# Head attention: the scores of two key tiles as four 32-row matmuls side by side, then twelve value products

## The chip, the cores and the metric

The kernel runs on one core of one Trainium2 chip. The metric is the device time of one execution in microseconds, the median over the runs shown. Lower is better.

## The reference

The program is a small network on x of 4 x 1024 tokens with 128 features: a mixture-of-experts layer, **head attention**, a second mixture-of-experts layer, a recurrent layer, a decayed attention with an MLP, and a recurrent layer again. The change lies in head attention alone, which the reference states so (`x` is already the layer norm of the residual stream, and the result is added to it):

```python
def _L0_attn_ref(x, weight):            # x: 4, 1024, 128
    nh = 16
    hs = c // nh                        # 8
    y = x.reshape(b, t, nh, hs).transpose(0, 2, 1, 3)
    scores = jnp.einsum('bhtk,bhsk->bhts', y, y) / math.sqrt(hs)
    attn = jax.nn.softmax(scores, axis=-1)
    o = jnp.einsum('bhts,bsc->bhtc', attn, x)
    return o.transpose(0, 2, 1, 3).reshape(b, t, nh * c) @ weight
```

So there are 4 x 16 = 64 heads of 8 dimensions. Each makes a 1024 x 1024 matrix of weights, which multiplies all 128 features of x, and each head's result of 128 x 1024 goes through its own 128 x 128 block of `weight` into the sum.

## The kernel before

Features lie on the 128 partitions, tokens along the free dimension. Single precision is rebuilt from two parts: every operand is split into a high part (rounded to the matmul's input type) and a low part (the rest), and `product` (L89 to L94) does three matmuls: low x high, high x low, high x high. Its lines L92, L93 and L94 are those that the profile names for value and output products.

`head_attention` first runs a layer norm (lines below L300, labelled `heads_norm`), which also writes the high and low parts to DRAM (`heads_parts`). Then comes one block in which the engines run their own programs, written out by hand and joined by semaphores. The work is 64 heads (`COUNT`), numbered h, of 8 key tiles of 128 keys (`TILES`), numbered s; n = 8h + s counts the tiles. The 1024 queries are two halves of 512, one PSUM bank each.

- **SP** (the queue that issues DMAs). `load_head(h)` (L722 to L728) fetches the operands of the scores of head h: 8 dimensions have 8 high and 8 low rows, 16 rows of 1024 numbers, and two such sets lie in `left` (high, low; high, low) and two in `right` (high, low; low, high), so that 32 rows carry all four products of parts. That is four DMAs of 64 KB (L727). The other 96 partitions of both tiles hold zeros, set once by GpSimd (L888, L889), for which SP waits before the first load. In the loop over heads SP waits for the reciprocals of head h (`inverse_ready`), stores them to DRAM in four DMAs (L737), waits until the scores of head h are done, loads head h+2, waits until the stores have landed, and loads the reciprocals back, broadcast to all partitions, as `scale` (L744).
- **TensorE**, step n: `scores(h, s)` (two matmuls, one for each half, L766) into one of two pairs of PSUM banks; where s is 7 and h at least 2, `add_head(h-2)`, the output product of a finished head (six matmuls); and then `weighted_rows` for the tile seven steps back (`TRAIL = 7`), six matmuls of the value product into the two OUT banks. Tile 0 of a head waits until the row products of the head before have read these banks (`scaled_ready`).
- **ScalarE**: the exponential of a tile (L817, 1024 columns at once, with the sum over queries in `accum_out`), where s is 0, 2, 4 or 6 (`ACT_HIGH`) also its high part (L822), and at the end of a head the high parts of u for the head before (L807). There are four buffers of exponentials; tile n waits for the low part of tile n - 4.
- **VectorE**: the high part of the other tiles (L871), the low part of all (L873). Behind tile 5 (`TRAIL - 2`) of head h it waits for the scale and for the last value product of head h-1 and multiplies the two (`scale_sums`, the row products u, L841); behind tile 7 the low parts of u (L847); and before tile 0 of the next head the reciprocals of the sums (L831) and their transpose (L834), which signals `inverse_ready`.

The attention is symmetric in its scores, so that the sum over queries of a key's row equals the sum that the softmax needs for that key as a query; this is why the scale comes after the value product.

Of the kernel before, what the change touches and what calls it, by code (L numbers as in the profile page):

```python
# [16 lines left out]
P = 128  # L17
BATCH, T = 4, 1024
TOKENS = BATCH * T
BANK = 512  # L20
CHUNKS = TOKENS // BANK
HALVES = T // BANK
# [10 lines left out]
HEADS, HEAD = 16, 8  # L33
TILES = T // P
# [24 lines left out]
def after(eng, sem, count):  # L59

    if isinstance(count, int) and count <= 0:
        return
    eng.wait_ge(sem, count)
# [9 lines left out]
def f(ap):  # L73

    return ap.bitcast(F32)
# [590 lines left out]
def head_attention(nc, tag, psum, consts, dram, x):  # L666


    with ExitStack() as ctx:
        sb, sem = sb_in(ctx, nc), sems_in(ctx, nc, tag)  # L670
# [6 lines left out]
        parts_dram = nc.dram_tensor(f"{tag}_parts", (P, 3, TOKENS), F32, kind="Internal").ap()  # L677
# [15 lines left out]

        zeroed, heads_loaded = sem("zeroed"), [sem("heads_even"), sem("heads_odd")]
        turned, v_by_act, v_by_dve = sem("turned"), sem("v_by_act"), sem("v_by_dve")
# [6 lines left out]
        sum_done, added = sem("sum_done"), sem("added")  # L702
        HEAD_LOADS = 4
        ACT_HIGH = (0, 2, 4, 6)
        TRAIL = 7
        COUNT = BATCH * HEADS
# [12 lines left out]
        with nc.Block() as block:  # L719
            @block.sync  # L720
            def _(sp):
                def load_head(h):  # L722
                    at = slice(h // HEADS * T, (h // HEADS + 1) * T)
                    dims = slice(h % HEADS * HEAD, (h % HEADS + 1) * HEAD)
                    for tile, orders in ((left, (0, 0)), (right, (0, 1))):
                        for i, order in enumerate(orders):
                            sp.dma_start(f(tile[i * 2 * HEAD:(i + 1) * 2 * HEAD, h % 2, :]),  # L727
                                         parts_dram[dims, order:order + 2, at]).then_inc(heads_loaded[h % 2], 16)  # L728

                sp.wait_ge(zeroed, 2)  # L730
                load_head(0)
# [16 lines left out]
            def _(pe):  # L748
# [11 lines left out]

                def scores(h, s):
                    if s == 0:
                        pe.wait_ge(heads_loaded[h % 2], 16 * HEAD_LOADS * (h // 2 + 1))
                    after(pe, exp_done, h * TILES + s - 1)
                    for half in range(HALVES):
                        last = pe.matmul(psum[:, SCORES + 2 * (s % 2) + half, :], left[:, h % 2, s * P:(s + 1) * P],  # L766
                                         right[:, h % 2, half * BANK:(half + 1) * BANK], start=True, stop=True)
                    last.then_inc(scores_done, 1)

# [20 lines left out]
                pe.wait_ge(v_by_dve, VALUE_BANKS)  # L790
                for n in range(COUNT * TILES + TRAIL):
                    if n < COUNT * TILES:
                        scores(n // TILES, n % TILES)
                    if n % TILES == TRAIL and n // TILES >= 2:
                        add_head(n // TILES - 2)
                    if n >= TRAIL:
                        weighted_rows((n - TRAIL) // TILES, (n - TRAIL) % TILES)
                for g in (COUNT - 2, COUNT - 1):
# [29 lines left out]
            def _(dve):  # L828
# [32 lines left out]
                for n in range(COUNT * TILES):  # L861
# [11 lines left out]
                    dve.tensor_tensor(e_lo[:, s, :], e[:, s % 4, :], f(e_hi[:, s, :]), ALU.subtract).then_inc(low, 1)  # L873
                    if s == TRAIL - 2 and h >= 1:
                        scale_sums(h - 1)
# [8 lines left out]
                dve.wait_ge(added, BATCH * HALVES)  # L884

            @block.gpsimd
            def _(pool):
                pool.memset(f(right[:, :, :]), 0.0).then_inc(zeroed, 1)  # L888
                pool.memset(f(left[:, :, :]), 0.0).then_inc(zeroed, 1)  # L889

# [685 lines left out]
```

## Time and profile before

| | |
|---|---|
| median of 3 runs | 3015.69 us (3014.63 to 3017.92) |
| the profiled execution | 3016.72 us, span 3014.9 us |
| busy over the span: TensorE, VectorE, ScalarE, GpSimd | 89%, 77%, 60%, 32% |
| head attention, first scores to last row products | 697 to 1727 us |
| mean granted TensorE clock, whole span | 0.929 |

The span is the time from the first to the last instruction on the core. A granted clock of 1 is 2.4 GHz, 0.5 is 1.2 GHz, and a number between is a mean over time. Matmuls are pipelined: a row with x2 merges two that overlap, and the time of one says less than the distance between starts. "PEld" is the weight load of TensorE, which runs beside its matmuls. "SPq" rows are DMA issues: the time that the queue's sequencer takes to issue one, not the transfer. In a view of waits, the name behind the arrow is what ended the wait.

### The profile page before, as it was taken

How to read it: one execution, taken by the hardware profiler on the slowest of the kernel's cores; microseconds unless marked ns; L12 is line 12 of the kernel's file. 1: busy time of each engine (PE TensorE's matmuls, PEld its weight loads, DVE VectorE, ACT ScalarE, POOL GpSimd, SP SyncE). 2: the span in 40 equal slices, each digit the busy share in tenths (PEclk: the TensorE clock that was granted, in tenths of full speed). 3: DMA queues.
4: the chain of work that ended last, by engine and by line, in shares of the span. 5: the costliest groups of instructions: out<-in, count | busy, mean ns of one | idle time of the engine just before them, and what ended most of it. 6: DMA issues, size and time to landing. Idle time of an engine off the chain costs nothing. (4 is left out here: it accounts for less than half of the span.)

```text
span 3014.9 us, 37679 instructions
## 1 busy us (share of the span) xinstructions
PE 2673.9 (89%) x11635; PEld 2163.0 (72%) x11635; DVE 2308.4 (77%) x3342; ACT 1804.5 (60%) x2927; POOL 965.2 (32%) x761
## 2 busy tenths in 40 slices
PE   7799999988999999999999978999999884555678
PEld 5688777866888888888888756887878663344456
DVE  6677777867999999999999776777877547776555
ACT  3355554547888888888888634555545443443365
POOL 2466666650000000000000034666666403444310
PEclk8899999998999999999999988999999886777788
DMA  1566655632111111111111106665656000000000
GB/s 55 128 142 132 152 123 122 146 99 76 44 52 53 50 46 53 53 45 51 53 53 43 46 25 144 132 151 126 147 128 140 21 22 28 14 14 0 8 7 28
DMA packets 76820, 222.76 MB, mean 74 GB/s; under 512 B 12145, under 2 KB 16881, under 8 KB 76529
## 3 DMA queue, kind: packets, MB, share of 16 engines
q1 hardware_dynamic: 76432, 220.77, 29.7%
q8 instruction: 70, 1.15, 0.2%
q14 instruction: 94, 0.76, 0.1%
q10 hardware_dynamic: 224, 0.07, 0.0%
HBM read 205.87 MB, written 10.75 MB: 72 GB/s over the span
## 5 line engine op out<-in xcount | busy, mean ns | idle before, releaser
L629 POOL TENSOR_TENSOR moe_experts_lo<-moe_experts_hidden,moe_experts_hi 128x512 fp32r<-128x512 f32 x512 | 662.3, 1294 | 388.3 <-ACT moe_experts_hi L567 388.3
L873 DVE TENSOR_TENSOR heads_e_lo<-heads_e,heads_e_hi 128x1024 fp32r<-128x1024 f32 x512 | 624.4, 1220 | 75.3 <-ACT heads_e_hi L822 66.4
L817 ACT ACTIVATE heads_e<-psum 128x1024 f32<-128x1024 f32 x512 | 525.0, 1025 | 131.2 <-PE psum L766 131.1
L574 ACT ACTIVATE psum<-psum 128x512 f32<-128x512 f32 x512 | 298.0, 582 | 493.6 <-PE psum L94 493.6
L601 DVE TENSOR_TENSOR moe_experts_weighted<-moe_experts_spread,psum 128x512 f32<-128x512 f32 x512 | 351.3, 686 | 238.2 <-PE psum L94 181.2
L92 PE MATMUL psum<-moe_n_hi,moe_w_lo 128*128 128x512 f32 x1024 | 406.2, 397 | 38.0 <-DVE moe_experts_hidden L606 34.2
L93 PE MATMUL psum<-moe_n_lo,moe_w_hi 128*128 128x512 f32 x1024 | 404.5, 395 | 0.0
L94 PE MATMUL psum<-moe_n_hi,moe_w_hi 128*128 128x512 f32 x1024 | 403.9, 394 | 0.0
L92 PE MATMUL psum<-heads_e_hi,heads_v_lo 128*128 128x512 f32 x1024 | 400.5, 391 | 0.7 <-DVE heads_u L841 0.7
L94 PE MATMUL psum<-heads_e_hi,heads_v_hi 128*128 128x512 f32 x1024 | 399.5, 390 | 0.0
L93 PE MATMUL psum<-heads_e_lo,heads_v_hi 128*128 128x512 f32 x1024 | 399.1, 390 | 0.0
L606 DVE TENSOR_TENSOR moe_experts_hidden<-moe_experts_weighted,psum 128x512 f32<-128x512 f32 x512 | 352.0, 687 | 34.3 <-POOL moe_experts_lo L629 16.9
L282 POOL CAST moe_router_hi<-moe_norm_raw 128x128 fp32r<-128x128 f32 x2 | 0.6, 291 | 1058.3 <-DMA moe_norm_raw<-in_router 1058.3
L567 ACT CAST moe_experts_hi<-moe_experts_hidden 128x512 fp32r<-128x512 f32 x512 | 314.0, 613 | 34.9 <-DVE moe_experts_hidden L606 34.9
L766 PE MATMUL psum<-heads_right,heads_left 128*128 128x512 f32 x1024 | 318.7, 393 | 4.8 <-ACT heads_e L817 3.9
L822 ACT CAST heads_e_hi<-heads_e 128x1024 fp32r<-128x1024 f32 x256 | 269.6, 1053 | 8.1
L92 PEld LDWEIGHTS psum<-moe_n_hi,moe_w_lo 128*128 128x128 f32 x1024 | 195.8, 191 | 84.0 <-DVE moe_experts_hidden L606 38.1
L766 PEld LDWEIGHTS psum<-heads_right,heads_left 128*128 128x128 f32 x1024 | 192.8, 189 | 48.0 <-ACT heads_e L817 7.4
L94 PEld LDWEIGHTS psum<-moe_n_hi,moe_w_hi 128*128 128x128 f32 x1024 | 195.9, 191 | 41.4
L93 PEld LDWEIGHTS psum<-moe_n_lo,moe_w_hi 128*128 128x128 f32 x1024 | 196.1, 192 | 40.8
L92 PEld LDWEIGHTS psum<-heads_e_hi,heads_v_lo 128*128 128x128 f32 x1024 | 192.6, 188 | 42.6 <-DVE heads_e_lo L873 1.1
L94 PEld LDWEIGHTS psum<-heads_e_hi,heads_v_hi 128*128 128x128 f32 x1024 | 192.5, 188 | 41.2
(426 smaller groups left out, 4527.2 us busy)
## 6 DMA issues: line engine op xcount, KB each, us to landing
moe_experts_spread<-moe_mask SPq DMA_DIRECT2D x128, 1024.0 KB, 11.5
heads_scale<-heads_inverse_copy SPq DMA_DIRECT2D x64, 512.0 KB, 3.7
heads_left<-heads_parts SPq DMA_DIRECT2D x128, 64.0 KB
heads_right<-heads_parts SPq DMA_DIRECT2D x128, 64.0 KB
moe_experts_raw<-in_gate SPq DMA_DIRECT2D x16, 256.0 KB, 12.0
moe_experts_raw<-in_up SPq DMA_DIRECT2D x16, 256.0 KB
moe_experts_raw<-in_down SPq DMA_DIRECT2D x16, 256.0 KB
heads_parts<-heads_e_hi SPq DMA_DIRECT2D x16, 256.0 KB, 3.2
```

What stands on the lines that cost most here:

```text
L92: pe.matmul(out, w_lo, x_hi, start=first, stop=False, skip_group_check=True)
L93: pe.matmul(out, w_hi, x_lo, start=False, stop=False, skip_group_check=True)
L94: return pe.matmul(out, w_hi, x_hi, start=False, stop=last, skip_group_check=True)
L567: act.copy(hi[:, p, :], hidden[:, p % 2, :]).then_inc(high_ready, 1)
L574: act.activation(psum[:, GATE + p % 2, :], psum[:, GATE + p % 2, :], ACT.Silu).then_inc(silu_ready, 1)
L601: dve.tensor_tensor(weighted[:, p % 2, :], spread[:, pair % 2, p, j * BANK:(j + 1) * BANK], psum[:, UP + p % 2, :], ALU.mult).then_inc(wei ...
L606: dve.tensor_tensor(hidden[:, p % 2, :], weighted[:, p % 2, :], psum[:, GATE + p % 2, :], ALU.mult).then_inc(hidden_ready, 1)
L629: pool.tensor_tensor(lo[:, p, :], hidden[:, p % 2, :], f(hi[:, p, :]), ALU.subtract).then_inc(low_ready, 1)
L766: last = pe.matmul(psum[:, SCORES + 2 * (s % 2) + half, :], left[:, h % 2, s * P:(s + 1) * P], right[:, h % 2, half * BANK:(half + 1) * BA ...
L817: act.activation(e[:, s % 4, :], wide, ACT.Exp, scale=HEAD ** -0.5, accum_out=sums[:, h % 2, s:s + 1]).then_inc(exp_done, 1)
L822: act.copy(e_hi[:, s, :], e[:, s % 4, :]).then_inc(act_high, 1)
L873: dve.tensor_tensor(e_lo[:, s, :], e[:, s % 4, :], f(e_hi[:, s, :]), ALU.subtract).then_inc(low, 1)
```

## The change

Four things change, all inside the block of `head_attention`.

1. `left` and `right` get four copies of the 32 operand rows, on partitions 0, 32, 64 and 96, in place of one copy and zeros. `load_head` issues 16 DMAs in place of 4, all of the old shape (`HEAD_LOADS = 16`). The memsets and the wait for them go.
2. TensorE goes by pairs of tiles. `scores` makes four matmuls, two tiles by two halves, each with 32 rows of the array of its own (`rows`) and a PSUM bank of its own, and now waits until both tiles of the pair before have been read by the exponential. Behind them stand the value products of two tiles, twelve matmuls, six and five tiles back (`TRAIL = 6`); `add_head` stands behind the scores of tiles 6 and 7.
3. ScalarE makes the high parts of the odd tiles, VectorE those of the even ones.
4. VectorE's row products stand behind tile 5 as before (`TRAIL - 1`).

```diff
--- before.py
+++ after.py
@@ -691,7 +691,7 @@
         u_hi, u_lo = sb(f"{tag}_u_hi", [P, 2, HALVES, BANK], F32R), sb(f"{tag}_u_lo", [P, 2, HALVES, BANK], F32R)
         SCORES, OUT, SUM = 0, 4, 6
 
-        zeroed, heads_loaded = sem("zeroed"), [sem("heads_even"), sem("heads_odd")]
+        heads_loaded = [sem("heads_even"), sem("heads_odd")]
         turned, v_by_act, v_by_dve = sem("turned"), sem("v_by_act"), sem("v_by_dve")
         scores_done, exp_done, dve_high, act_high, low = (
             sem("scores"), sem("exp"), sem("dve_high"), sem("act_high"), sem("low"))
@@ -700,9 +700,9 @@
         scale_loaded = [sem("scale_even"), sem("scale_odd")]
         out_done, scaled_ready, u_high, u_low = sem("out"), sem("scaled"), sem("u_high"), sem("u_low")
         sum_done, added = sem("sum_done"), sem("added")
-        HEAD_LOADS = 4
-        ACT_HIGH = (0, 2, 4, 6)
-        TRAIL = 7
+        HEAD_LOADS = 16
+        ACT_HIGH = (1, 3, 5, 7)
+        TRAIL = 6
         COUNT = BATCH * HEADS
         VALUE_BANKS = TOKENS // BANK
 
@@ -724,10 +724,11 @@
                     dims = slice(h % HEADS * HEAD, (h % HEADS + 1) * HEAD)
                     for tile, orders in ((left, (0, 0)), (right, (0, 1))):
                         for i, order in enumerate(orders):
-                            sp.dma_start(f(tile[i * 2 * HEAD:(i + 1) * 2 * HEAD, h % 2, :]),
-                                         parts_dram[dims, order:order + 2, at]).then_inc(heads_loaded[h % 2], 16)
-
-                sp.wait_ge(zeroed, 2)
+                            for g in range(4):
+                                row = 32 * g + i * 2 * HEAD
+                                sp.dma_start(f(tile[row:row + 2 * HEAD, h % 2, :]),
+                                             parts_dram[dims, order:order + 2, at]).then_inc(heads_loaded[h % 2], 16)
+
                 load_head(0)
                 load_head(1)
                 for h in range(COUNT):
@@ -759,13 +760,17 @@
                     last.then_inc(sum_done, 1)
 
                 def scores(h, s):
+
                     if s == 0:
                         pe.wait_ge(heads_loaded[h % 2], 16 * HEAD_LOADS * (h // 2 + 1))
-                    after(pe, exp_done, h * TILES + s - 1)
-                    for half in range(HALVES):
-                        last = pe.matmul(psum[:, SCORES + 2 * (s % 2) + half, :], left[:, h % 2, s * P:(s + 1) * P],
-                                         right[:, h % 2, half * BANK:(half + 1) * BANK], start=True, stop=True)
-                    last.then_inc(scores_done, 1)
+                    after(pe, exp_done, h * TILES + s)
+                    for tile in (s, s + 1):
+                        for half in range(HALVES):
+                            g = 2 * (tile % 2) + half
+                            rows = slice(32 * g, 32 * (g + 1))
+                            last = pe.matmul(psum[:, SCORES + g, :], left[rows, h % 2, tile * P:(tile + 1) * P],
+                                             right[rows, h % 2, half * BANK:(half + 1) * BANK], start=True, stop=True)
+                        last.then_inc(scores_done, 1)
 
                 def weighted_rows(h, s):
                     pe.wait_ge(low, h * TILES + s + 1)
@@ -788,13 +793,14 @@
                     last.then_inc(turned, 1)
                 pe.wait_ge(v_by_act, VALUE_BANKS)
                 pe.wait_ge(v_by_dve, VALUE_BANKS)
-                for n in range(COUNT * TILES + TRAIL):
+                for n in range(0, COUNT * TILES + TRAIL, 2):
                     if n < COUNT * TILES:
                         scores(n // TILES, n % TILES)
-                    if n % TILES == TRAIL and n // TILES >= 2:
-                        add_head(n // TILES - 2)
                     if n >= TRAIL:
-                        weighted_rows((n - TRAIL) // TILES, (n - TRAIL) % TILES)
+                        if n % TILES == TRAIL and n // TILES >= 2:
+                            add_head(n // TILES - 2)
+                        for m in (n - TRAIL, n - TRAIL + 1):
+                            weighted_rows(m // TILES, m % TILES)
                 for g in (COUNT - 2, COUNT - 1):
                     add_head(g)
 
@@ -871,7 +877,7 @@
                         dve.tensor_copy(e_hi[:, s, :], e[:, s % 4, :]).then_inc(dve_high, 1)
                         dve.wait_ge(dve_high, high_dve)
                     dve.tensor_tensor(e_lo[:, s, :], e[:, s % 4, :], f(e_hi[:, s, :]), ALU.subtract).then_inc(low, 1)
-                    if s == TRAIL - 2 and h >= 1:
+                    if s == TRAIL - 1 and h >= 1:
                         scale_sums(h - 1)
                     if s == TILES - 1 and h >= 1:
                         u_lows(h - 1)
@@ -882,11 +888,6 @@
                 u_lows(COUNT - 1)
                 add_batch(BATCH - 1)
                 dve.wait_ge(added, BATCH * HALVES)
-
-            @block.gpsimd
-            def _(pool):
-                pool.memset(f(right[:, :, :]), 0.0).then_inc(zeroed, 1)
-                pool.memset(f(left[:, :, :]), 0.0).then_inc(zeroed, 1)
 
 
 def recurrent_layer(nc, tag, psum, consts, dram, x, out=None):
```

On TensorE, this stood where a head's last scores are followed by the output product of an older head (`heads_u`, `heads_w`) and the first value product of its own (`heads_e`, `heads_v`), before:

```order
L766 MATMUL psum<-heads_right,heads_left 128x512 x2
L92 MATMUL psum<-heads_e_hi,heads_v_lo 128x512
L93 MATMUL psum<-heads_e_lo,heads_v_hi 128x512
L94 MATMUL psum<-heads_e_hi,heads_v_hi 128x512
L92 MATMUL psum<-heads_e_hi,heads_v_lo 128x512
L93 MATMUL psum<-heads_e_lo,heads_v_hi 128x512
L94 MATMUL psum<-heads_e_hi,heads_v_hi 128x512
L766 MATMUL psum<-heads_right,heads_left 128x512 x2
L92 MATMUL psum<-heads_u_hi,heads_w_lo 128x512
```

and now, the four scores of tiles 6 and 7 and the six matmuls of the output product behind them:

```order
L771 MATMUL psum<-heads_right,heads_left 128x512 x4
L92 MATMUL psum<-heads_u_hi,heads_w_lo 128x512
L93 MATMUL psum<-heads_u_lo,heads_w_hi 128x512
L94 MATMUL psum<-heads_u_hi,heads_w_hi 128x512
L92 MATMUL psum<-heads_u_hi,heads_w_lo 128x512
L93 MATMUL psum<-heads_u_lo,heads_w_hi 128x512
L94 MATMUL psum<-heads_u_hi,heads_w_hi 128x512
L92 MATMUL psum<-heads_e_hi,heads_v_lo 128x512
```

Scores came two at a time between six products; they now come four at a time between twelve, or eighteen where the output product stands.

On the SP queue, the loads of heads 0 and 1 and then the loop's first head, before:

```order
L727 DMA heads_left<-heads_parts 16x1x1024 x2
L727 DMA heads_right<-heads_parts 16x1x1024 x2
L727 DMA heads_left<-heads_parts 16x1x1024 x2
L727 DMA heads_right<-heads_parts 16x1x1024 x2
L737 DMA heads_inverse_copy<-heads_inverse_rows 8x32 x4
L727 DMA heads_left<-heads_parts 16x1x1024 x2
L727 DMA heads_right<-heads_parts 16x1x1024 x2
L744 DMA heads_scale<-heads_inverse_copy 128x1024
```

and now:

```order
L729 DMA heads_left<-heads_parts 16x1x1024 x8
L729 DMA heads_right<-heads_parts 16x1x1024 x8
L729 DMA heads_left<-heads_parts 16x1x1024 x8
L729 DMA heads_right<-heads_parts 16x1x1024 x8
L738 DMA heads_inverse_copy<-heads_inverse_rows 8x32 x4
L729 DMA heads_left<-heads_parts 16x1x1024 x8
L729 DMA heads_right<-heads_parts 16x1x1024 x8
L745 DMA heads_scale<-heads_inverse_copy 128x1024
```

Between the stores of a head's reciprocals and the load of its scales stand 16 loads in place of 4. The order of the three kinds is the same.

On VectorE, from a head's row products (`heads_u`) to the transpose that ends the next, now:

```order
L847 TENSOR_TENSOR heads_u<-heads_scale,psum 128x512 x2
L877 CAST heads_e_hi<-heads_e 128x1024
L879 TENSOR_TENSOR heads_e_lo<-heads_e,heads_e_hi 128x1024 x2
L853 TENSOR_TENSOR heads_u_lo<-heads_u,heads_u_hi 128x512 x2
L837 RECIPROCAL heads_inverse<-heads_sums 128x8
L840 STREAM_TRANSPOSE heads_inverse_rows<-heads_inverse 128x32
```

Before, the same instructions stood there, with the cast between the two low parts.

## Rows read from the trace of the kernel before

**Rows 1.** Busy time by engine inside head attention: stretch, us, then PE, PEld, DVE, ACT, POOL.

```profile
720.00:1700.00 980.00, 979.34 (x4299) 806.41 (x4298) 909.07 (x1112) 845.40 (x1354) 0.00 (x0) 1.00 0.15 50
```

**Rows 2.** Waits by engine and line, 720 to 1700 us: total us, times, longest.

```profile
ACT heads_e L817 <- PE psum L766: 126.9, 246, 0.9
DVE heads_e_lo L873 <- ACT heads_e_hi L822: 60.3, 116, 0.5
```

**Rows 3.** Timeline of TensorE at 1214 us: start, us, instruction, count.

```profile
1214.02 0.39 PE L93 MATMUL psum<-heads_e_lo,heads_v_hi 128*128 128x512 f32 x1
1214.25 0.39 PE L94 MATMUL psum<-heads_e_hi,heads_v_hi 128*128 128x512 f32 x1
1214.47 0.62 PE L766 MATMUL psum<-heads_right,heads_left 128*128 128x512 f32 x2
1214.93 0.39 PE L92 MATMUL psum<-heads_e_hi,heads_v_lo 128*128 128x512 f32 x1
```

**Rows 4.** Timeline of VectorE: row products, end of a head, next row products.

```profile
1202.60 1.28 DVE L841 TENSOR_TENSOR heads_u<-heads_scale,psum 128x512 f32<-128x512 f32 x2
...
1208.23 0.21 DVE L834 STREAM_TRANSPOSE heads_inverse_rows<-heads_inverse 128x32 f32<-128x32 f32 x1
...
1218.56 1.28 DVE L841 TENSOR_TENSOR heads_u<-heads_scale,psum 128x512 f32<-128x512 f32 x2
```

**Rows 5.** Timeline of the SP queue, the same head.

```profile
1208.47 1.28 SPq L737 DMA_DIRECT2D heads_inverse_copy<-heads_inverse_rows  x4
1209.80 1.39 SPq L727 DMA_DIRECT2D heads_left<-heads_parts  x2
1211.23 1.35 SPq L727 DMA_DIRECT2D heads_right<-heads_parts  x2
1212.68 0.38 SPq L744 DMA_DIRECT2D heads_scale<-heads_inverse_copy  x1
```

**Rows 6.** Timeline of the weight loads at 1214 us.

```profile
1214.70 0.19 PEld L92 LDWEIGHTS psum<-heads_e_hi,heads_v_lo 128*128 128x128 f32 x1
```

**Rows 7.** Timeline of TensorE: one-column matmuls in a row, in the layer norm.

```profile
659.69 2.73 PE L208 MATMUL psum<-inv,heads_norm_squares 128*128 128x1 f32 x24
```

**Rows 8.** The tile of left operands: its load issues, ns min/median/max.

```profile
L727 SPq DMA_DIRECT2D heads_left<-heads_parts x128: 654/670/1155, 690.7 to 1689.4; - x128
```

**Rows 9.** The DRAM copy of the reciprocals: issues, ns min/median/max, and landing, us.

```profile
L737 SPq DMA_DIRECT2D heads_inverse_copy<-heads_inverse_rows x256: 263/288/917, 713.0 to 1719.8; - x128
L744 SPq DMA_DIRECT2D heads_scale<-heads_inverse_copy x64: 342/382/444, 717.2 to 1721.0; - x64
...
DMA to landing us min/median/max: 3.3/3.7/5.5
```

**Rows 10.** Line L834: the transpose that ends a head, ns, first and last start us.

```profile
L834 DVE STREAM_TRANSPOSE heads_inverse_rows<-heads_inverse x64: 211/211/213, 712.8 to 1718.6; 128x32 f32<-128x32 f32 x64
```

**Rows 11.** Timeline of the SP queue: the first eight loads, two pairs of four shown.

```profile
690.73 1.53 SPq L727 DMA_DIRECT2D heads_left<-heads_parts  x2
...
695.10 1.35 SPq L727 DMA_DIRECT2D heads_right<-heads_parts  x2
```

**Rows 12.** Waits of the SP queue, whole span: the one before the first load.

```profile
SPq L727 <- POOL heads_left L889: 3.6, 1, 3.6
```

**Rows 13.** DMA issues: a 64 KB load of another layer, KB, median us to landing.

```profile
cell_norm_raw<-in_wi SPq DMA_DIRECT2D x2, 64.0 KB, 2.0
```

**Rows 14.** Timeline of TensorE: the first scores, and what it waited for.

```profile
697.30 1.17 PE L766 MATMUL psum<-heads_right,heads_left 128*128 128x512 f32 x4 [0.83 <-ACT heads_v_lo L811]
```

**Rows 15.** Timeline of TensorE: after a long wait in the first layer.

```profile
105.97 0.80 PE L92 MATMUL psum<-moe_n_hi,moe_w_lo 128*128 128x512 f32 x1 [8.29 <-DVE moe_experts_hidden L606]
```

**Rows 16.** Stretches behind that wait: the column after POOL is the granted clock.

```profile
106.00:113.00 7.00, 7.00 (x20) 5.57 (x21) 3.95 (x6) 2.78 (x5) 2.92 (x3) 0.63 1.02 210
113.00:120.00 7.00, 7.00 (x33) 5.79 (x32) 4.51 (x7) 3.71 (x7) 4.75 (x4) 1.00 0.14 35
```

## The prediction

> **What bounds the kernel now.** I read the busy time by stretch first. Between 720 and 1700 us, inside head attention, TensorE is busy 979.34 of 980 us at a granted clock of 1.00, while VectorE has 909.07 and ScalarE 845.40 [rows 1]. So TensorE sets the pace of this stage. The waits say the same: ScalarE waits 126.9 us for scores and VectorE 60.3 us for ScalarE's high parts [rows 2], and TensorE has no wait worth a row. The transpose that ends a head starts first at 712.8 and, for the 64th head, at 1718.6 [rows 10]: (1718.6 - 712.8) / 63 = 15.97 us is the period of a head.
>
> The view that decides the forecast is the SP queue, since the change puts four times as many loads there. In one head [rows 5]: the transpose of VectorE starts at 1208.23 and takes 0.21 [rows 4], so the reciprocals are ready at 1208.44. SP issues four stores from 1208.47, then the four loads of head h+2 from 1209.80, and only then, at 1212.68, the broadcast load of the scales of head h. It lands 3.7 us after its issue (3.3 to 5.5) [rows 9], so at 1216.38. VectorE needs it for its row products at 1218.56 [rows 4]. **The slack is 2.2 us a head.** The reader should see that this queue is idle most of the time (from 1213.1 until the next head's stores, one period after 1208.47), and that nevertheless its latency lies 2.2 us under the critical path.
>
> **TensorE's part.** In a row, matmuls of 512 columns start 0.227 us apart, products and scores alike: 1214.02, 1214.25, 1214.47 for the first of two scores, 1214.93 for what follows both [rows 3]. A head has 48 value products, 6 output products and 16 score matmuls: 70 x 0.227 = 15.9 us, the measured period. The change makes the 16 into four groups of four on separate rows. No row shows such a group, so I bound its time S from both sides. Below: all four side by side cost one distance, 0.227. Above: nothing overlaps. The rest of the last product runs out (0.39 - 0.227 = 0.16), a weight load takes 0.19 [rows 6], the four start 0.227 apart (0.68), the last takes 0.39 and the next product's weight load 0.19: 1.61. Weight loads and one-column matmuls in a row go at 2.73 / 24 = 0.114 us each [rows 7], so between the ends I take four starts 0.114 apart with the weight loads hidden, about 0.45. TensorE's work per head is then 54 x 0.227 + 4S = 12.3 + 1.8 = 14.1 us, with ends of 13.2 and 18.7, against 15.9 now.
>
> The Trainium skill (TensorEngine Tiling (Array Packing), Key Properties) says that a change of tiling mode drains TensorE, and this change switches eight times a head. Worked out with drains on both sides and overlapping matmuls, S is 0.16 + 0.19 + 3 x 0.114 + 0.39 + 0.19 = 1.27 and a head 17.3 us, slower than now instead of faster. No run here shows such a switch between row groups. Whether 14.1 or 17.3, the sum below stays as it is, since something else takes 22.2 us; the rule decides only if that falls away, and there it is a rival.
>
> **VectorE and ScalarE.** Their instructions per head are the same (four high parts each; the even ones move to VectorE, the odd to ScalarE). Priced at nothing, covered by the stall found below: its cover is several us a head. VectorE's own floor is 15.97 less its waits, 60.3 us over 980 / 15.97 = 61.4 heads, 0.98: 14.99 us.
>
> **The SP queue.** A load issue takes 0.670 us (654 to 1155 ns) [rows 8], and eight in a row went from 690.73 to 696.45, 0.715 each with a long first one [rows 11]; in the steady head two take 1.43 and 1.35. I take 0.70. Each of the 16 new loads has the shape of the old ones, 16 rows of 4 KB, so twelve more issues are 12 x 0.70 = **8.4 us** ahead of the scale load. The waits for stored reciprocals and for free buffers that stand between them are over long before, and cost nothing. From reciprocals ready to scales landed:
> 0.03 + 1.33 (stores) + 2.88 (four loads) + 8.4 + 3.7 = 16.3 us, where it was 7.9.
>
> Now who waits. VectorE does its row products of head h behind its sixth tile of head h+1, as before. They are due 10.1 us after the reciprocals (1208.44 to 1218.56); the scales come at 16.3. In order behind them stand the tiles 6 and 7 of head h+1, the low parts of u and the reciprocals of head h+1, and only these release the next stores on SP. That is a closed loop. Its VectorE part is read off directly: row products at 1202.60, reciprocals ready at 1208.44, with no gap between, 5.84 us for the same instructions as after the change (one cast, two low parts, two of u, the reciprocal). With 0.05 for the wake-up the period is 16.3 + 0.05 + 5.84 = **22.2 us** a head instead of 15.97.
>
> Does anything else in this loop take longer? TensorE waits for the scaled rows before the first value product of head h+1, and must have done the last one before the next row products. That chain is 0.7 (first row product) + 48 x 0.227 + 3S = 0.7 + 10.9 + 1.4 = 13 us, 16.4 with S at 1.61. But TensorE will now idle 6 to 8 us each head. After a wait of 8.29 us [rows 15] the next 7 us had a mean granted clock of 0.63 [rows 16], which is 1.2 GHz for 74% of it, 5.2 us, and 2.4 GHz after that; 5.2 us of work at half the rate lose 2.6. So 16 us, at most 19, against 22.2: it is covered by 3 us or more. VectorE's tiles 4 and 5 hang on three groups of products: 0.7 + 3 x (2.72 + 0.45) + 2.6 + 1 for cold scores, then 2.3 for two exponentials, 1.1 for a cast and 1.2 for a low part, 18.4 us: covered too.
>
> **Start and end.** The memsets on GpSimd go, with the SP wait of 3.6 us for them [rows 12], so the first load is issued at 690.73 - 3.6 = 687.1. But head 0 now needs 16: the last is issued at 687.1 + 15 x 0.70 = 697.6 and lands 2.0 later (as a 64 KB load elsewhere [rows 13]), at 699.6, where scores begin at 697.30 now [rows 14]. With the scores exposed in pairs in that first head I take +3 us. The last two heads have no loads in front of their scales; between -1 and +4, I take +1.
>
> **Sum.** 62 heads have loads in front of their scales. 62 x (22.2 - 15.97) = 386; with 3 and 1, +390. The profiled execution took 3016.72 us (span 3014.9), so 3407, and the median of the runs is 1.0 lower: **3406 us**, 13% slower. A measurement of this kernel can tell 0.2%, 6 us, from no change.
>
> **Rivals.**
> 1. *The scales come later still*, or a chain through TensorE closes the loop. For it: the loads move 1 MB in 11 us right in front of the scale load, whose landing already varies to 5.5, and TensorE's margin is the smallest cover. Against: the scale load follows loads back to back today and lands in 3.7. At 5.5 each time the period is 24.0: 3016 + 62 x 8.0 + 4 = 3516. A TensorE held at half rate would need 48 x 0.454 + 3 x 1.7 + 0.7 = 27.6 us (3740), but then it wouldn't idle. Chance 0.12.
> 2. *Issues are cheaper in a long burst.* The nearest cheap rows are the scale issue at 0.382 and the stores at 0.288 [rows 9]. At 0.32, twelve are 3.8 us and the period 17.7: about 3125. Against: eight loads in a row went no faster than two. Chance 0.05, and 0.01 more that it just comes out even.
> 3. *The other side: the queue stays under the path* and TensorE's saving shows. That needs twelve issues within the slack, under 2.2 / 12 = 0.18 us each, where the shortest load is 0.654. Then VectorE bounds at 14.99: 3016 - 64 x 0.98 = 2953. The Trainium skill (TensorE: Matmul & The Clock Gate, Measured speedup vs the span model) gives 3.07 times for four row tiles of 512 columns, which would let that saving through; it says nothing of the queue. Chance 0.02.
> 4. *The drains bind*, by the rule above, with the queue out of the way: 3016 + 64 x (17.3 - 15.97) = 3101. Chance 0.01.
> 5. *The four matmuls don't run side by side.* Then S is 0.9 and nothing of the forecast changes; it is inside it.
>
> **How the numbers follow.** Forecast 0.79, rival 1 0.12, rival 2 0.05 and 0.01, rivals 3 and 4 0.02 and 0.01. The forecast's own ends: 0.66 an issue and 3.3 to land give 21.35 us a head and 3353; 0.715 with 4.5 to land gives 23.2 and 3468. Reaching into rival 1, the range is 3358 to 3505. Faster 0.02, within 0.2% 0.01, slower 0.97.
>
> **What would show it.** In the changed profile: the end-of-head transposes 22 us apart; SP with 16 loads in about 11.2 us between stores and scale issue; VectorE idle some 6 us before each row product, released by the scale load; TensorE at 60 to 70% busy in this stage with its idle time before a head's first value product, and a mean clock below 1. Wrong would be: issues under 0.6 us, row products released by TensorE, or a period under 20.

## The result, and the profile after

| | before | after |
|---|---|---|
| median of 4 runs | 3015.16 us (3014.28 to 3017.92) | 3413.43 us (3408.85 to 3421.34) |
| profiled execution, span | 3016.72, 3014.9 us | 3408.85, 3407.1 us |
| ratio, 95% interval | | 1.1322 (1.1299 to 1.1344) |
| period of a head, mean of the first 62 | 15.97 us | 22.33 us |

The change makes the kernel 13% slower. The forecast was 3406 us, range 3358 to 3505. The medians are of executions in the chip's usual state; one of the four of the version with one row group further down ran in a slower one, 3328.12 us at a mean granted clock of 0.807, and is left out of its median.

The page of the changed kernel, parts 1 and 2, shows no engine that got much more to do; TensorE is less busy and its clock lower in the stage:

```profile
PE 2745.8 (81%) x11635; PEld 2079.8 (61%) x11635; DVE 2338.4 (69%) x3342; ACT 1811.0 (53%) x2927; POOL 961.8 (28%) x759
...
PEclk8899999878888888888888889899999988677788
```

The same view as [rows 1], over the stretch 760 to 2050 us (stretch, its length, then busy PE, PEld, DVE, ACT, POOL, and the granted clock):

```profile
760.00:2050.00 1290.00, 997.79 (x4049) 688.31 (x4050) 881.03 (x1043) 802.51 (x1275) 0.00 (x0) 0.88 0.23 72
```

TensorE is busy 77% of the stage where it was 99.9%. The waits by engine and line, the view of [rows 2], name the chain:

```profile
PE psum L92 <- DVE heads_u L847: 292.2, 58, 6.4
ACT heads_e L823 <- PE psum L771: 289.8, 232, 5.1
DVE heads_u L847 <- DMA heads_scale<-heads_inverse_copy: 271.3, 58, 6.1
```

VectorE waits for the scale load before its row products, TensorE waits for the row products before a head's first value product, and ScalarE waits for the scores that stand behind that in TensorE's program. Of the three, the profile before had the wait of ScalarE, with 126.9 us over 980 [rows 2], that of TensorE once, with 0.7 us, and that of VectorE not at all. The tile of scales says how often, and how long its DMA takes:

```profile
  DMA heads_scale<-heads_inverse_copy: 291.0, 62
...
DMA to landing us min/median/max: 3.3/3.7/4.4
```

VectorE waited 62 times, once for each head that has loads in front of its scales, and the landing is as before, 3.7 us [rows 9]. One head on the SP queue, against [rows 5]:

```profile
1229.82 1.29 SPq L738 DMA_DIRECT2D heads_inverse_copy<-heads_inverse_rows  x4
1231.15 5.58 SPq L729 DMA_DIRECT2D heads_left<-heads_parts  x8
1236.77 5.54 SPq L729 DMA_DIRECT2D heads_right<-heads_parts  x8
1242.40 0.38 SPq L745 DMA_DIRECT2D heads_scale<-heads_inverse_copy  x1
1251.98 1.29 SPq L738 DMA_DIRECT2D heads_inverse_copy<-heads_inverse_rows  x4
```

and VectorE in the same head, against [rows 4]:

```profile
1246.11 1.28 DVE L847 TENSOR_TENSOR heads_u<-heads_scale,psum 128x512 f32<-128x512 f32 x2 [4.05 <-DMA heads_scale<-heads_inverse_copy]
...
1251.75 0.21 DVE L840 STREAM_TRANSPOSE heads_inverse_rows<-heads_inverse 128x32 f32<-128x32 f32 x1
```

The loop can be read off and closes: stores at 1229.82, loads at 1231.15 (1.33), scales at 1242.40 (11.25), row products at 1246.11 (3.71), reciprocals ready at 1251.96 (5.85), the next stores at 1251.98. That is 22.16 us. Over the whole stage the transpose that ends a head [rows 10] has

```profile
L840 DVE STREAM_TRANSPOSE heads_inverse_rows<-heads_inverse x64: 211/211/214, 714.7 to 2116.0; 128x32 f32<-128x32 f32 x64
```

and the 63rd of them starts at 2099.05, so 62 periods are 1384.3 us, 394.4 more than before. With the later first transpose (1.9 us) and 4.2 us less from the 63rd transpose to the end, that is the whole difference of the spans: 3014.9 + 1.9 + 394.4 - 4.2 = 3407.0.

What TensorE gained is there too, against [rows 3]:

```profile
1209.84 0.39 PE L94 MATMUL psum<-heads_e_hi,heads_v_hi 128*128 128x512 f32 x1
1210.16 0.51 PE L771 MATMUL psum<-heads_right,heads_left 32*128 32x512 f32 x4
1210.60 0.50 PE L92 MATMUL psum<-heads_e_hi,heads_v_lo 128*128 128x512 f32 x1
1210.93 0.39 PE L93 MATMUL psum<-heads_e_lo,heads_v_hi 128*128 128x512 f32 x1
```

Four matmuls of 512 columns take 0.51 us together. From the last product before them to the second one behind them it is 1.09 us; less the two distances of 0.227 that would be there anyway, a group costs S = 0.64 us, where four in a row cost 0.91. Two delays are seen in it: the group starts 0.32 us after the last product and not 0.227, and the second product follows the first 0.33 later. The weight loads of the group start with its matmuls:

```profile
1210.15 0.19 PEld L771 LDWEIGHTS psum<-heads_right,heads_left 32*128 32x128 f32 x4 [0.35 <-issue]
```

The tile of left operands shows the weight loads, the matmuls, and the same load issues as [rows 8]:

```profile
L771 PEld LDWEIGHTS psum<-heads_right,heads_left x1024: 181/181/284, 700.3 to 2108.9; 32*128 32x128 f32 x171
L771 PE MATMUL psum<-heads_right,heads_left x1024: 467/497/791, 700.3 to 2108.9; 32*128 32x512 f32 x171
L729 SPq DMA_DIRECT2D heads_left<-heads_parts x512: 654/655/1372, 686.8 to 2083.2; - x171
```

The clock around one of the waits (last number before the DMA columns), against [rows 16]; TensorE was idle in the first stretch:

```profile
1195.70:1201.50 5.80, 0.00 (x0) 0.03 (x1) 0.83 (x2) 1.62 (x4) 0.00 (x0) 0.85 0.40 124
1201.50:1206.70 5.20, 5.20 (x12) 3.79 (x12) 4.95 (x8) 1.10 (x2) 0.00 (x0) 0.52 0.00 0
1206.70:1219.00 12.30, 12.30 (x59) 8.34 (x58) 9.44 (x9) 11.02 (x18) 0.00 (x0) 1.00 0.25 73
```

Behind the wait TensorE runs at 1.2 GHz for nearly 5.2 us (mean 0.52) and then at 2.4 GHz again (mean 1.00).

### The profile page after: what moved, and what is told of

Same layout as the page of the kernel before. It is cut to its first block and busy times, and to the rows that moved or that the text cites. A ratio compares the mean times of both kernels' runs of the same rounds, so it can differ in the third digit from the quotient of the medians.

```text
span 3407.1 us, 38445 instructions
## 1 busy us (share of the span) xinstructions
PE 2745.8 (81%) x11635; PEld 2079.8 (61%) x11635; DVE 2338.4 (69%) x3342; ACT 1811.0 (53%) x2927; POOL 961.8 (28%) x759
## 5 line engine op out<-in xcount | busy, mean ns | idle before, releaser
L92 PE MATMUL psum<-heads_e_hi,heads_v_lo 128*128 128x512 f32 x1024 | 480.8, 470 | 315.0 <-DVE heads_u L847 315.0
L92 PEld LDWEIGHTS psum<-heads_e_hi,heads_v_lo 128*128 128x128 f32 x1024 | 220.0, 215 | 430.6 <-issue 357.3
L93 PE MATMUL psum<-heads_e_lo,heads_v_hi 128*128 128x512 f32 x1024 | 450.8, 440 | 0.0
L94 PE MATMUL psum<-heads_e_hi,heads_v_hi 128*128 128x512 f32 x1024 | 447.0, 437 | 0.0
L847 DVE TENSOR_TENSOR heads_u<-heads_scale,psum 128x512 f32<-128x512 f32 x128 | 82.3, 684 | 297.2 <-DMA heads_scale<-heads_inverse_copy 291.0
L877 DVE CAST heads_e_hi<-heads_e 128x1024 fp32r<-128x1024 f32 x256 | 177.2, 692 | 117.6 <-ACT heads_e L823 108.2
L94 PEld LDWEIGHTS psum<-heads_e_hi,heads_v_hi 128*128 128x128 f32 x1024 | 222.2, 217 | 56.3
L93 PEld LDWEIGHTS psum<-heads_e_lo,heads_v_hi 128*128 128x128 f32 x1024 | 223.3, 218 | 41.6
```

Of the source, the lines that this page charges most:

```text
L92: pe.matmul(out, w_lo, x_hi, start=first, stop=False, skip_group_check=True)
L93: pe.matmul(out, w_hi, x_lo, start=False, stop=False, skip_group_check=True)
L94: return pe.matmul(out, w_hi, x_hi, start=False, stop=last, skip_group_check=True)
L877: dve.tensor_copy(e_hi[:, s, :], e[:, s % 4, :]).then_inc(dve_high, 1)
```

## The experiments

The theory was that the queue closes a loop, and that nothing else in the change bears on the time. Its rivals were the new order on TensorE with its switches to 32 rows, and a cost of 16 loads that is not their issue. Each ratio is to the kernel before on the same chip, whose medians are 3012.75 to 3016.48 us. Periods are from here on the mean of all 63, from the first transpose to the 64th; so taken, the change has (2116.0 - 714.7) / 63 = 22.24 us.

**The extra loads alone, without the change.**

```diff
 # kernel before
-        HEAD_LOADS = 4
+        HEAD_LOADS = 16
+                            for g in range(1, 4):
+                                row = 32 * g + i * 2 * HEAD
+                                sp.dma_start(spare[row:row + 2 * HEAD, int(tile is right), h % 2, :],
+                                             parts_dram[dims, order:order + 2, at]).then_inc(heads_loaded[h % 2], 16)
```

> The kernel before with the twelve extra loads alone: same shape and source, same place on the SP queue, their target a tile that nobody reads. TensorE's program is that of before. Theory: period 7.94 + 12 x 0.70 + 0.05 + 5.84 = 22.2 us as in the change, time 3400 to 3420. Rival (TensorE's part is the cost): 3016, since transfers that nobody reads cost nothing.

Measured: 3419.72 us, ratio 1.1339 (1.1316 to 1.1361). The two views of it that count, waits and the transpose (L839 here):

```profile
DVE heads_u L846 <- DMA heads_scale<-heads_inverse_copy: 276.6, 57, 6.4
```

```profile
L839 DVE STREAM_TRANSPOSE heads_inverse_rows<-heads_inverse x64: 211/211/214, 718.3 to 2126.8; 128x32 f32<-128x32 f32 x64
```

(2126.8 - 718.3) / 63 = 22.36 us a head, and the time lies at the upper end of the 3400 to 3420 expected. Twelve loads that nobody reads cost what the whole change costs, with TensorE's program untouched. The theory stands, and the rival that makes TensorE the cause is out.

**Fewer loads, with the change.** The loads that stay keep their place ahead of the scales, and GpSimd zeroes the tiles as before the change. These two versions leave out the scores of the row groups that hold zeros, so they serve for times alone.

```diff
 # the change
-                            for g in range(4):
+                            for g in range(1):     # e4: range(2)
-        HEAD_LOADS = 16
+        HEAD_LOADS = 4                             # e4: 8
```

> The change with 8 loads a head (row groups 0 and 1; groups 2 and 3 hold zeros, so half of the score matmuls are left out). Theory: four extra loads make the loop 7.94 + 2.8 + 0.05 + 5.84 = 16.6 us, just over the other engines, so 3016.7 + 62 x (16.6 - 15.97) + 3 = 3059 (3045 to 3075). If the loop had slack left, or overlapped with something, it would be 2950 to 2990 as with 4 loads.

> The change with 4 loads a head in place of 16, in their old place ahead of the scales: the operands come to partitions 0 to 31 alone, the other three row groups hold zeros, so that this leaves the scores of three matmuls in four out. The instructions of all engines but SP are those of the change. Theory: the loop is 7.94 + 0.05 + 5.84 = 13.8 us, under VectorE's 14.99, so the same 2950 to 2990 as with the scales first. Rival: above 3300.

Measured with 8 loads: 3063.84 us, ratio 1.0159 (1.0138 to 1.0179); with 4: 2989.4 us, ratio 0.9907 (0.9890 to 0.9923). The transpose in the first and in the second:

```profile
L841 DVE STREAM_TRANSPOSE heads_inverse_rows<-heads_inverse x64: 211/211/215, 713.4 to 1767.2; 128x32 f32<-128x32 f32 x64
```

```profile
L841 DVE STREAM_TRANSPOSE heads_inverse_rows<-heads_inverse x64: 211/211/214, 713.8 to 1694.5; 128x32 f32<-128x32 f32 x64
```

Both times are in the ranges expected, the second at its upper end. The periods are 16.73 and 15.57 us. So 16, 8 and 4 loads give 22.24, 16.73 and 15.57: eight loads cost 5.5 us a head, 0.69 each, as long as the queue is the bound, and between 8 and 4 another bound takes over. With 4 loads the rest of the change is a gain of 0.9%.

**The scales ahead of the loads.**

```diff
 # the change, SP's loop
+                    sp.wait_ge(inverse_stored, 16 * (P // 32) * (h + 1))
+                    after(sp, scaled_ready, (h - 1) * HALVES)
+                    sp.dma_start(scale...).then_inc(scale_loaded[h % 2], 16)
                     if h + 2 < COUNT:
                         sp.wait_ge(scores_done, (h + 1) * TILES)
                         load_head(h + 2)
-                    sp.wait_ge(inverse_stored, 16 * (P // 32) * (h + 1))
-                    after(sp, scaled_ready, (h - 1) * HALVES)
-                    sp.dma_start(scale...).then_inc(scale_loaded[h % 2], 16)
```

> The change, with the load of the scales put ahead of the 16 loads of head h+2 on the SP queue. Theory (the queue closes the loop): from reciprocals ready to scales landed it is now 0.03 + 1.33 + 0.9 (the stores must land, as in the two heads without loads before) + 3.7 = 6.0 us, the loop 6.0 + 0.05 + 5.84 = 11.9 us, and no longer the bound. VectorE's 14.99 and TensorE's 54 x 0.227 + 4 x 0.64 = 14.8 are. Period 15.0 to 15.5, time 2950 to 2990, faster than both kernels. Rival (the change is slow because of the new order on TensorE and its switches to 32 rows, the queue only goes along): period above 20, time above 3300. Middle rival (both count): between 3016 and 3300.

Measured: 3101.33 us, ratio 1.029 (1.0273 to 1.0308), period 17.23 us. That is the middle rival's range, not mine. The wait for the scales is gone, as the theory says, but another has come. Waits, the SP queue in one head, and TensorE at the first scores of the next but one:

```profile
PE psum L771 <- DMA heads_right<-heads_parts: 73.1, 39, 4.1
```

```profile
1218.10 1.29 SPq L738 DMA_DIRECT2D heads_inverse_copy<-heads_inverse_rows  x4
1220.28 0.35 SPq L742 DMA_DIRECT2D heads_scale<-heads_inverse_copy  x1
1220.67 5.57 SPq L729 DMA_DIRECT2D heads_left<-heads_parts  x8
1226.29 5.54 SPq L729 DMA_DIRECT2D heads_right<-heads_parts  x8
```

```profile
1233.77 0.80 PE L771 MATMUL psum<-heads_right,heads_left 32*128 32x512 f32 x4 [2.22 <-DMA heads_right<-heads_parts]
```

The issue of the last load ends at 1231.8, 13.7 us after the first store's began, and TensorE can start the scores of that head at 1233.77, 15.7 us after it. I had moved the loads and had followed only what they no longer delay. Each head's loads still begin with the reciprocals of the head two before, and TensorE needs them about when the next reciprocals are due.

**Two ways to let the loads land earlier.** The first sends half of them through GpSimd:

```diff
 # scales ahead of the loads, and on SP only the left tile's
+            @block.gpsimd
+            def _(pool):
+                for h in range(COUNT):
+                    if h >= 2:
+                        pool.wait_ge(scores_done, (h - 1) * TILES)
+                    ...
+                            pool.dma_start(f(right[row:row + 2 * HEAD, h % 2, :]),
+                                           parts_dram[dims, order:order + 2, at]).then_inc(right_loaded[h % 2], 16)
```

> The change with the scales first on SP, the 8 loads of the left tile behind them on SP, and the 8 of the right tile issued by GpSimd, which is idle in this stage and waits for the scores itself. Theory: in the run with the scales first the head's loads came 15.8 us after the reciprocals and TensorE waited for them (73 us in 39 waits); here they come at 2.7 + 5.6 + 2 = 10.3, under every other bound, so the period is that of the run with 4 loads, 15.57 us, and the time 2980 to 3000. Rival (another cost of 16 loads, such as the transfers' use of memory or of the DMA engines): stays at 3050 or more.

The second keeps all on SP, in an order that uses its idle time before the reciprocals:

```diff
 # scales ahead of the loads
+                    if h + 2 < COUNT:
+                        sp.wait_ge(scores_done, (h + 1) * TILES)
+                        load_head(h + 2, ((left, (0, 0)),))
                     sp.wait_ge(inverse_ready, h + 1)
                     ...
                     if h + 2 < COUNT:
-                        sp.wait_ge(scores_done, (h + 1) * TILES)
-                        load_head(h + 2)
+                        load_head(h + 2, ((right, (0, 1)),))
```

> All on SP, in a third order: the 8 loads of the left tile ahead of the wait for the reciprocals (the scores of head h are done some 5 us before its reciprocals), then stores, scales, and the 8 loads of the right tile. Theory: the stores start at most 1 us late, scales land at 0.6 + 2.7 + 3.7 = 7 us, the last load at 0.6 + 2.7 + 5.6 + 2 = 11 us, both under their bounds: 2980 to 3000 as with two queues. If what costs is the number of issues on this queue (13.9 us of 15.6), it will be above that, 3020 or more.

Measured: 2986.81 us (ratio 0.9912, 0.9896 to 0.9929) and 2990.04 us (0.9928, 0.9911 to 0.9945). Both are in the range expected and reach the time with 4 loads (2984.77 to 2991.17 there, 2986.24 to 2994.34 here), so the transfers of 16 loads cost nothing that these runs can tell; the loads cost by where their issues stand on the queue. The rival is out, and so is the one that blames the number of issues on SP.

**What the four matmuls are worth.** Two runs with 4 loads, both with the new order of four scores and twelve products. In the first all four use the same 32 rows, in the second all 128 rows with zeros, as in the kernel before.

```diff
-                            rows = slice(32 * g, 32 * (g + 1))
+                            rows = slice(0, 32)    # e6: slice(0, P)
```

> The new order with 4 loads a head and all four score matmuls of a pair on rows 0 to 31, one after the other, in their own banks. Theory (side by side is worth three distances of 0.227 a group, and the switch to 32 rows costs what the trace of the change shows): S = 0.65 + 0.68 = 1.33 us in place of 0.65, TensorE 12.4 + 4 x 1.33 = 17.7 us a head, period 17.7 to 18.2, time 3130 to 3165. Rival (matmuls on different row groups are not what makes the group short): as with 4 loads and four groups, 2989.

> The new order (four scores, then twelve products) with 4 loads a head and scores on all 128 rows, zeros under the operands, as in the kernel before: no row groups and no switch. Theory: S = 4 x 0.227 = 0.91, TensorE 12.4 + 3.6 = 16.0 us a head plus a little waiting at a head's first product, period 16.0 to 16.4, time 3016 to 3045; so the order in pairs alone gains nothing, and row groups save 0.91 - 0.65 = 0.26 us a group. Rival (the gain of the run with 4 loads comes from the pairs, or from ScalarE's other tiles): 2989 or less.

Measured: 3123.68 us (ratio 1.037, 1.0349 to 1.0391) and 3015.12 us (1.0008, 0.9999 to 1.0018), the first 6 us and the second 1 us below the ranges expected. Both rivals are out. TensorE's timeline around a group, on one row group:

```profile
1201.11 0.39 PE L94 MATMUL psum<-heads_e_hi,heads_v_hi 128*128 128x512 f32 x1
1201.42 1.20 PE L771 MATMUL psum<-heads_right,heads_left 32*128 32x512 f32 x4
1202.55 0.50 PE L92 MATMUL psum<-heads_u_hi,heads_w_lo 128*128 128x512 f32 x1
1202.89 0.40 PE L93 MATMUL psum<-heads_u_lo,heads_w_hi 128*128 128x512 f32 x1
```

the last three of its four scores by themselves:

```profile
1201.76 0.86 PE L771 MATMUL psum<-heads_right,heads_left 32*128 32x512 f32 x3
```

and on all rows:

```profile
1199.56 0.39 PE L94 MATMUL psum<-heads_e_hi,heads_v_hi 128*128 128x512 f32 x1
1199.79 1.07 PE L772 MATMUL psum<-heads_right,heads_left 128*128 128x512 f32 x4
1200.69 0.40 PE L92 MATMUL psum<-heads_u_hi,heads_w_lo 128*128 128x512 f32 x1
1200.93 0.40 PE L93 MATMUL psum<-heads_u_lo,heads_w_hi 128*128 128x512 f32 x1
```

Read as above, S is 1.78 - 0.45 = 1.33 us and 1.37 - 0.45 = 0.92 us. So by the rows going to 32 rows and back costs 0.41 us a group, running side by side saves 0.69 (1.33 - 0.64), and 0.28 is left, 1.1 us a head. The 0.41 lies at the two switches, about 0.1 on each side of either: the four scores on one row group start at 1201.42, 1201.76, and the other two 0.23 us apart each ((0.86 - 0.39) / 2), the first product at 1202.55 and the second at 1202.89. So the gaps are 0.31, 0.34, 0.23, 0.23, 0.33 and 0.34, against 0.23 in a row without switches. Side by side, one gap of 0.227 and the 0.41 of the switches make the 0.64 measured. The weight loads of the group, on one row group and on all rows, show one thing that changes at the switch:

```profile
1201.42 0.76 PEld L771 LDWEIGHTS psum<-heads_right,heads_left 32*128 32x128 f32 x4 [0.35 <-issue]
```

```profile
1199.56 0.87 PEld L772 LDWEIGHTS psum<-heads_right,heads_left 128*128 128x128 f32 x4
```

Without a switch the first weight load starts at 1199.56, with the product before the group and 0.23 us ahead of its own matmul; with one it starts at 1201.42, together with its own matmul.

The periods check these prices, since TensorE is busy for at least 889 of 890 us (760 to 1650) in the three runs compared: all rows, one row group, and four row groups in the split-load run with early row products, which follows below.

```profile
L841 DVE STREAM_TRANSPOSE heads_inverse_rows<-heads_inverse x64: 211/211/213, 710.1 to 1717.8; 128x32 f32<-128x32 f32 x64
```

```profile
L840 DVE STREAM_TRANSPOSE heads_inverse_rows<-heads_inverse x64: 211/212/215, 711.4 to 1827.6; 128x32 f32<-128x32 f32 x64
```

```profile
L842 DVE STREAM_TRANSPOSE heads_inverse_rows<-heads_inverse x64: 211/213/216, 714.3 to 1663.0; 128x32 f32<-128x32 f32 x64
```

They are 15.99, 17.72 and 15.06 us. By them the switches cost 0.43 us a group, running side by side saves 0.66, and 0.23 is left, 0.9 us a head, somewhat less than the rows of one group say. The order in pairs alone is worth nothing. The Trainium skill (TensorEngine Tiling (Array Packing), Key Properties) has the drain at a mode change as a rule without a price. These rows agree that a switch costs something, 0.41 us a group; the 1.27 us that I worked out for a group with drains on both sides was twice the 0.64 measured.

**The next wait.** In the two-queue run TensorE still stood still once a head (all engines' timeline):

```profile
1207.28 1.28 DVE L849 TENSOR_TENSOR heads_u<-heads_scale,psum 128x512 f32<-128x512 f32 x2
...
1207.49 0.40 PE L94 MATMUL psum<-heads_u_hi,heads_w_hi 128*128 128x512 f32 x1
...
1208.11 0.47 PE L92 MATMUL psum<-heads_e_hi,heads_v_lo 128*128 128x512 f32 x1 [0.22 <-DVE heads_u L849]
```

From 1207.49 to 1208.11 are 0.62 us, 0.39 more than a distance, while VectorE starts on the row products that free the banks.

```diff
-                    if s == TRAIL - 1 and h >= 1:
+                    if s == TRAIL - 2 and h >= 1:
                         scale_sums(h - 1)
```

> The split loads on SP, with VectorE's row products behind tile 4 of a head in place of tile 5. Theory: with two queues or split loads each head still loses 0.39 us on TensorE between the output product and the first value product (1207.49 to 1208.11, against a distance of 0.23), because VectorE reaches the row products only behind the low part of tile 5; the last value product that they wait for ends at 1205.85, when the low part of tile 4 is about done. So the row products start at about 1206.0 and TensorE's wait goes: 62 x 0.39 = 24 us, 2960 to 2972. Rival (VectorE now waits for the value product, or is the bound itself with 15.0 a head): 2980 or more.

> The two-queue version with the row products behind tile 4. Same theory and numbers, 2958 to 2970; if it differs from the run with split loads by more than 5 us, the full SP queue (13.9 us of a head of 15.2) has become a bound there.

Measured: 2960.47 us (0.9816, 0.9800 to 0.9833) with split loads and **2957.78 us (0.9803, 0.9787 to 0.9820)** with two queues, the first just inside its range and the second 0.2 us below it. Busy time of the first over 760 to 1650 us, and the transpose in the second:

```profile
760.00:1650.00 890.00, 890.00 (x4146) 626.52 (x4145) 875.68 (x1076) 812.71 (x1304) 0.00 (x0) 1.00 0.34 105
```

```profile
L842 DVE STREAM_TRANSPOSE heads_inverse_rows<-heads_inverse x64: 211/213/216, 714.7 to 1665.7; 128x32 f32<-128x32 f32 x64
```

With split loads TensorE is busy 890 of 890 us again, at 15.06 us a head; with two queues a head takes (1665.7 - 714.7) / 63 = 15.10 us. Their ranges overlap (2958.11 to 2963.94 and 2954.39 to 2960.75), so neither is shown to be the faster. They are the fastest versions here and take 1.8% and 2.0% less time than the kernel before.

## Why the prediction was right

- *TensorE bounds the kernel before, the SP queue lies 2.2 us under the path.* Right. With four extra loads' issue (2.8 us) the queue is the bound and the period 16.73, for which the loop's terms give 7.94 + 2.8 + 0.05 + 5.84 = 16.6; with none it is not.
- *Twelve loads at 0.70 add 8.4 us.* Right. The 16 took 11.25 where 2.88 + 8.4 = 11.28 was forecast.
- *Landing 3.7, VectorE's part 5.84, loop 22.2.* 3.71, 5.85 and, on the mean of 62 heads, 22.33. Some heads are longer than the one shown, by a load issue or a landing (up to 4.4). From the first store's issue to that of the scales it is 12.58 us in the head shown and 12.67 in the mean of 62, and from there to the row products 3.71 and 3.78; that is the difference.
- *S = 0.45 with weight loads hidden, ends 0.227 and 1.61.* Too low, 0.64. The step that failed is "with the weight loads hidden, starts 0.114 apart": the weight loads of the group start with its own matmuls, 0.31 us behind the start of the last product, and the first product behind the group is followed 0.33 later. The matmuls themselves run closer together than I took: four take 0.51 us, of which one alone takes 0.47 or more. It changed nothing in the sum, as forecast, since TensorE had cover.
- *TensorE idles 6 to 8 us a head and loses 2.6 us to the clock.* The idle time is less, 292.2 us in 58 heads or 5.0 each, since I had not taken the slow stretch and the larger S off it. For the same reason the sign "60 to 70% busy" came out at 77%: 54 x 0.227 + 4 x 0.64 + 2.5 = 17.3 us of 22.33. The slow stretch is right: 5.2 us at a mean clock of 0.52 in the rows shown, a loss of 2.5.
- *VectorE idles some 6 us before the row products.* It waited 271.3 us in 58 heads there, 4.7 each; another 1.7 (96.0 us in the view below) went earlier in the head, to the exponentials. Together they make up the 6.

```profile
DVE heads_e_hi L877 <- ACT heads_e L823: 96.0, 58, 2.4
```

- *Start and end.* First load 686.8 (687.1), first scores 700.3 (699.6), first transpose 1.9 us later (+3); from the 63rd transpose to the end -4.2 (+1). Of that, 4.6 us lie in the layers behind head attention, which the change doesn't touch; that difference between two single executions I leave unexplained. Start and end together gave -2.3 us where +4 was forecast, and the 62 heads 394.4 where 386 was. The two errors, -6.3 and +8.4, cancel in part: that the profiled execution took 3408.85 us where 3407 was forecast is to that extent luck. The mechanism and the terms of the loop are not.
- *Rival 1* (scales later still) has the 0.1 us and no more. *Rival 2* didn't come: an issue took 0.70. *Rival 4* didn't either: the run with the scales first took its 3101 us, but by waiting for loads, and without that wait the time is 2987. *Rival 3* was right about its condition: with the queue out of the way TensorE's saving does show, and with one more wait removed it reaches 2958, near the 2953 that VectorE's floor gave. But TensorE sets the pace there and not VectorE: with split loads TensorE has no wait and most heads are 15.03 us apart, while the first three behind each later change of batch come 14.72 to 14.75 apart, so VectorE's floor is below the 14.99 worked out. *Rival 5*, no running side by side, is out: four scores take 0.51 us, against 1.20 on one row group.
- *The range.* Its lower end, 3358, lies above the 3353 that the prediction itself works out for the forecast's own lower case, without a reason. The result doesn't come near either.

## What to carry to other kernels

An idle queue can be the next bound. Look for what stands behind a group of issues on the same queue and at how much earlier its data lands than it is needed; here 2.2 us of slack met 8.4 us of issues, and the gain that the change was made of, 0.9 us a head on TensorE, could not be seen until they were moved. When work is moved on a queue, follow both what it no longer delays and what it now delays itself.

## What was not expected of the hardware

- A switch from 128-row to 32-row matmuls and back costs 0.41 us in a full stream (1.33 against 0.92 us a group; 0.43 by the periods), and four 512-column matmuls on four row groups take 0.51 us against 1.20 on one.
- The same 64 KB load costs GpSimd's queue less to issue than SP's 0.655 us median above. In the two-queue run with the row products behind tile 5:

```profile
L904 POOL DMA_DIRECT2D heads_right<-heads_parts x512: 542/562/1027, 688.3 to 1661.3; - x171
```

- A DMA of 512 KB to 128 partitions issues in 0.382 us, one of 64 KB to 16 partitions in 0.655: for these two shapes the issue doesn't go by bytes.
